# A state-space layer with a gated feed-forward: TensorE's column jobs in two halves, with one of a slot's two tiles of states transposed ahead of each

## The reference

```python
xn = _layernorm(x)
u, gate = split(xn @ W_in.T)                 # 1024 channels each
u = silu(causal_conv4(u) + conv_b)
dt, B, C = split(u @ Wx.T)                   # 32, 16, 16; each normalised (rms)
delta = softplus(dt @ Wdt.T + dt_bias)
state = exp(delta * A) * state + (delta * u) * B     # 1024 x 16 states, step by step
y = (sum over n of state * C + u * D_param) * silu(gate)
g = silu(ffn(xn))                            # gated feed-forward, 512 -> 1376 -> 512
out = x + (y @ W_out.T) * g
```

## Time and profile before

| what | value |
|---|---|
| median of three runs | 1201.54 us |
| the profiled execution | 1197.73 us, of which span 1195.9 us |
| PE busy | 1068.4 us (89%) |
| DVE busy | 1049.6 us (88%) |
| POOL busy | 1008.5 us (84%) |
| ACT busy | 710.2 us (59%) |
| granted TensorE clock, mean | 0.96 of full |

### The profile page before, as it was taken

One profiled execution on the slowest core, in us unless ns is written; L12 is line 12 of the kernel. 1 busy time (PEld: TensorE's weight loads), 2 busy tenths in 40 slices (PEclk: granted clock), 3 DMA queues, 4 the chain that ended last, 5 costly groups with the idle time before them and its releaser, 6 DMA issues.

```text
span 1195.9 us, 16709 instructions
## 1 busy us (share of the span) xinstructions
PE 1068.4 (89%) x5072; PEld 764.7 (64%) x5072; DVE 1049.6 (88%) x1248; ACT 710.2 (59%) x1155; POOL 1008.5 (84%) x542
## 2 busy tenths in 40 slices
PE   5979886888999979998997997998998999999767
PEld 4757665566657767675756786576756787555444
DVE  4478789899989999899987999899998999888985
ACT  4667646776574846577583665576576575464440
POOL 3589997999978898889977897879988889878961
PEclk9979998799999999999999998999999999999978
DMA  4537553443224443343322463424323443334410
GB/s 133 206 128 239 187 185 129 139 155 132 90 87 152 170 175 118 121 155 129 107 81 100 166 203 117 152 103 160 107 96 107 161 160 124 119 101 150 141 61 36
DMA packets 46566, 160.82 MB, mean 134 GB/s; under 512 B 5355, under 2 KB 5611, under 8 KB 37004
## 3 DMA queue, kind: packets, MB, share of 16 engines
q1 hardware_dynamic: 45424, 159.14, 38.9%
q10 hardware_dynamic: 1052, 0.59, 0.2%
HBM read 135.33 MB, written 24.38 MB: 134 GB/s over the span
## 4 chain that ended last, share of the span: by engine, by line
PE 47%; DVE 18%; POOL 16%; issue 14%; ACT 3%; DMA 1%; DVEq 1%; SPq 0%; POOLq 0%; ACTq 0%
PE pj L1068 15%; PE hT L1353 10%; DVE sb_h L1007 9%; POOL sb_dBu L770 8%; PE pj L1266 7%; DVE sb_yT L934 4%; PE pj L1300 4%; PE pj L1331 3%; POOL sb_yT L740 3%; PE pj L1086 2%; PE pj L1371 2%; DVE sb_un L855 2%; POOL sb_un L714 1%; POOL sb_w_sp L709 1%; PE pj L1073 1%
## 5 line engine op out<-in xcount | busy, mean ns | idle before, releaser
L770 POOL TENSOR_TENSOR sb_dBu<-sb_v,sb_bb 128x1024 f32<-128x1024 f32 x256 | 606.8, 2382 | 34.1 <-DVE sb_h L1007 26.6
L1007 DVE TENSOR_TENSOR_SCAN sb_h<-dA,sb_dBu 128x512 f32<-128x512 f32 x512 | 596.2, 1205 | 42.1 <-POOL sb_dBu L770 29.2
L581 ACT ACTIVATE dA<-sb_delta,sb_apar 128x512 f32<-128x512 f32 x512 | 345.0, 688 | 252.8 <-DVE sb_h L1007 248.6
L1068 PE MATMUL pj<-sb_x_hi,sb_w_sp 128*128 128x512 f32 x1208 | 347.6, 411 | 22.8 <-DVE sb_un L855 12.0
L1353 PE MATMUL hT<-sb_ident,sb_h 128*128 128x128 f32 x2048 | 290.0, 284 | 83.2 <-DVE sb_yT L934 68.1
L1353 PEld LDWEIGHTS hT<-sb_ident,sb_h 128*128 128x128 f32 x2048 | 244.4, 145 | 167.6 <-DVE sb_yT L934 52.9
L1068 PEld LDWEIGHTS pj<-sb_x_hi,sb_w_sp 128*128 128x128 f32 x1208 | 222.2, 194 | 85.4 <-issue 23.4
L934 DVE SCALAR_TENSOR_TENSOR sb_yT<-hT,sb_cs,sb_yT 128x512 f32<-128x512 f32 x321 | 228.4, 732 | 46.1 <-PE hT L1353 45.5
L740 POOL TENSOR_TENSOR sb_yT<-sb_yT,sb_part 128x512 f32<-128x512 f32 x155 | 198.8, 1283 | 68.0 <-ACT sb_part L674 67.8
L674 ACT ACTIVATE sb_part<-hT,sb_cs_act 128x512 f32<-128x512 f32 x155 | 106.0, 684 | 160.2 <-PE hT L1353 151.9
L1068 PE MATMUL pj<-sb_x_lo,sb_w_sp 128*128 128x512 f32 x604 | 167.6, 400 | 0.0
(11 more groups left out here) (119 smaller groups left out, 816.4 us busy)
## 6 DMA issues: line engine op xcount, KB each, us to landing
sb_w_sp<-w_cache SPq DMA_DIRECT2D x55, 1024.0 KB, 4.8
sb_ring<-w_ring SPq DMA_DIRECT2D x67, 512.0 KB, 3.4
sb_bb<-b_rows SPq DMA_DIRECT2D x128, 256.0 KB, 3.7
w_cache<-sb_w_sp SPq DMA_DIRECT2D x19, 1024.0 KB, 4.8
sb_xio<-x SPq DMA_DIRECT2D x7, 1024.0 KB, 7.2
out<-sb_xio SPq DMA_DIRECT2D x3, 1024.0 KB, 5.7
sb_xio<-x SPq DMA_DIRECT2D x4, 256.0 KB, 3.7
out<-sb_xio SPq DMA_DIRECT2D x4, 256.0 KB, 2.0
```

Source lines behind the costliest of these rows:

```text
L581: nc.scalar.activation(dA[g % 2][:, :], delta[:, j, :], ACT.Exp, scale=apar[:, j, n:n + 1]).then_inc(dA_done, 1)
L770: nc.gpsimd.tensor_tensor(dBu[:, dbu_buffer(s), :, :], v[:, j:j + 2, :], bb[:, i % B_RING, :].unsqueeze(1).to_broadcast([P, 2, T]), ALU.mu ...
L1007: nc.vector.tensor_tensor_scan(h[:, i % 2, 2 * part + e, :], dA[g % 2][:, :], dBu[:, dbu_buffer(s), e, :], 0.0, ALU.mult, ALU.add).then_in ...
L1068: done = nc.tensor.matmul(bank[:, :], w[:, kk * P:(kk + 1) * P], xs[:, kk, :], start=(p == 0), stop=(p == len(products) - 1))
```

## The change

`column(s)` gets a second argument `half` and is called twice. The slot is now: first tile, `misc(s)`, half 0 of the column; second tile, half 1. `misc` is not divided. Of a column from `x` a half is six of the twelve products, of the out-projection two of four, of the down-projection the first two and what is left. All waits of a column stand in half 0, all signals at the last product. The u column at slot 31 gets one wait more at its head, for the new `x` (`xT_done`). `tail(s)` is called whole in half 1.

```diff
-            def from_x(bank, buf, part, ready, new_x=None):
+            def from_x(bank, buf, part, ready, new_x=None, halves=(0, 1)):
                 hi, lo = w_hi[:, buf, part], w_lo[:, buf, part]
                 products = [(w, xs, kk) for w, xs in ((lo, x_hi), (hi, x_lo), (hi, x_hi)) for kk in range(KH)]
                 for p, (w, xs, kk) in enumerate(products):
+                    if p // 6 not in halves:
+                        continue
...
-                done.then_inc(ready, 1)
+                if 1 in halves:
+                    done.then_inc(ready, 1)
...
-                        for m in range(JH):
+                        for m in (2 * half, 2 * half + 1):
...
-                        if part == 1:
+                        if part == 1 and half == 1:
                             done.then_inc(op_ps, 1)
                     if last:
-                        tail(s)
+                        if half == 1:
+                            tail(s)
                         return
                     if s in U_AT:
                         j = U_AT.index(s)
...
+                        elif j == 0:
+
+                            pe.wait_ge(xT_done, (b + 1) * KH + 3)
...
                     if s in DOWN_AT:
                         e, ts = DOWN_AT[s]
+                        ts = ts[:2] if half == 0 else ts[2:]
...
                         done.then_inc(hT_ps, 1)
-                    misc(s)
-                    column(s)
+                        if c % 2 == 0:
+                            misc(s)
+                        column(s, c % 2)
```

More of the change, by code:

```diff
@@ L1216, in misc, with ffn @@
                         to_delta(b + 1, j, pj[3])
-                def ffn(c, q):
+                def ffn(c, q, half):
                     t, part = q // 2, q % 2
-                    if part == 0:
+                    if half == 0 and part == 0:
                         weights(c, FFN0 + t)
-                    if q < 3 and isinstance(c, int) and c == 0:
+                    if half == 1:
+                        pass
+                    elif q < 3 and isinstance(c, int) and c == 0:
                         pe.wait_ge(*[(sg_done, 3), (sg_done, 4), (del_done, 2)][q])
@@ L1232, in ffn, with column @@
                         pe.wait_ge(fs_done, c * KI + t)
-                    from_x(pj[q % 3], t % HI_RING, part, fu_ps if part else fg_ps)
-                def column(s):
+                    from_x(pj[q % 3], t % HI_RING, part, fu_ps if part else fg_ps, halves=(half,))
+                def column(s, half):
                     if s - q_ffn < 2 * KI:
-                        ffn(b, s - q_ffn)
+                        ffn(b, s - q_ffn, half)
                     if s >= SLOTS - LEAD and not last:
-                        ffn(b + 1, s - SLOTS + LEAD)
+                        ffn(b + 1, s - SLOTS + LEAD, half)
                     j = s - q_gate1 + JH
                     if JH <= j < KD:
-                        if j % 2 == 0:
+                        if half == 0 and j % 2 == 0:
                             weights(b, GATE1 + (j - JH) // 2)
-                        if j == JH:
+                        if half == 1:
+                            pass
+                        elif j == JH:
                             pe.wait_ge(f_done, (b + 1) * KI - 1)
@@ L1252, in column @@
                             pe.wait_ge(sg_done, b * KD + JH + 1)
-                        from_x(pj[(Q_GATE1 + j - JH) % 3], (GATE1 + (j - JH) // 2) % HI_RING, j % 2, gt_ps)
+                        from_x(pj[(Q_GATE1 + j - JH) % 3], (GATE1 + (j - JH) // 2) % HI_RING, j % 2, gt_ps, halves=(half,))
                     e, part = (s - S_OUT) // 2, (s - S_OUT) % 2
                     if 0 <= e < KH and not first:
-                        if part == 0:
+                        if part == 0 and half == 0:
                             weights(b, OUT0 + e)
@@ L1274, in column @@
                         j = U_AT.index(s)
-                        if j % 2 == 0:
+                        if half == 0 and j % 2 == 0:
                             weights(b, U0 + j // 2)
-                        if j == 1 and first:
+                        if half == 1:
+                            pass
+                        elif j == 0:
+                            pe.wait_ge(xT_done, (b + 1) * KH + 3)
+                        elif j == 1 and first:
                             pe.wait_ge(sg_done, 7)
@@ L1282, in column @@
                             pe.wait_ge(tap_done, ((b + 1) * KD + j - 1) * (KC - 1))
-                        from_x(pj[U_BANK[j % 2]], (GATE1 + 2 + j // 2) % HI_RING, j % 2, u_ps, (b + 1) * KH if j == 0 else None)
+                        from_x(pj[U_BANK[j % 2]], (GATE1 + 2 + j // 2) % HI_RING, j % 2, u_ps, (b + 1) * KH if j == 0 else None, (half,))
                     if s in DOWN_AT:
                         e, ts = DOWN_AT[s]
-                        if e == 0 and ts[0] == 0:
+                        ts = ts[:2] if half == 0 else ts[2:]
+                        if 0 not in ts:
+                            pass
+                        elif e == 0:
                             pe.wait_ge(f_done, (b + 1) * KI)
@@ L1291, in column @@
                                 pe.wait_ge(og_done, b * KH)
-                        elif e == 1 and ts[0] == 0:
+                        elif e == 1:
                             pe.wait_ge(g_done, b * KH + 1)
-                        elif ts[0] == 0:
+                        else:
                             pe.wait_ge(sg_done, (b + 1) * KD + e)
@@ L1306, in column @@
                         j = GATE0_AT.index(s)
-                        if j % 2 == 0:
+                        if half == 0 and j % 2 == 0:
                             weights(b, GATE0 + j // 2)
-                        if j < 2:
+                        if half == 1:
+                            pass
+                        elif j < 2:
                             pe.wait_ge(tap_done, ((b + 1) * KD + 7 + j) * (KC - 1))
@@ L1314, in column @@
                             pe.wait_ge(sg_done, (b + 1) * KD + 1)
-                        from_x(pj[GATE0_BANK[j]], (GATE1 + 6 + j // 2) % HI_RING, j % 2, gt_ps)
+                        from_x(pj[GATE0_BANK[j]], (GATE1 + 6 + j // 2) % HI_RING, j % 2, gt_ps, halves=(half,))
                 def tail(s):
```

## The result

The changed kernel took 1249.44 us (median of four runs, 1242.74 to 1251.28), against 1201.55 us for the kernel before: ratio 1.0394, interval 1.0355 to 1.0432, 48 us slower. Forecast were 1225 us and a range of 1203 to 1242. The direction and the place (VectorE standing behind late tiles) were right, the size (23 us) was half of what it is, and 1249 lies above the range.

A forecast was written before the change was run, and what follows sets the result against it. Three nearly full engines (TensorE 89%, VectorE 88%, GpSimd 84%), none bounding the whole alone. Terms of 7.05, twice 7.55 and 1.0 us summed to 23.2, giving 1224.7 beside the median; predicted 1225 us, range 1203 to 1242.

The forecast's parts named there:

- (a): Delta jobs of the first slots: VectorE waits for a later tile, 0.5 us a middle batch (bounds 0 and 1.6).
- (b): Start of the out-projection: second tile no longer done during a wait, 0.5 us a batch, none in the first.
- (c): From out-projection to taps, slot 33: tile 2.16 us later, VectorE full after it; 2.1 us a middle batch.
- (d): Inside the taps stretch, slots 35, 36 and 39: late second tiles, 1.8 us halved to 0.9 a middle batch.
- (e): Slots 47 and 48: 16 `to_ssm` products each ahead of the second tile, 2.9 us a middle batch (bounds 0 and 3.9).
- (f): Slots 55 to 57: delta job and two down products ahead of the tile, 1.3 us halved to 0.65 a middle batch.
- More alternations: Every slot: one more switch between transposes and products on TensorE, costed at zero, at most 28 us.
- The wait that goes: TensorE's 20 waits ahead of four transposes, 18.6 us together, could go; net effect taken as about zero.
- would show it: Expected signs: VectorE's wait for transposes from 45.5 to 80 us or more, about 2.5 us of wait in slot 33.
- more than the sum: Rival: unhalved terms plus 1.2 GHz stretches after TensorE's waits, signed by four transposes taking 0.66 us; 1239 us, chance 0.13.
- the ScalarE reserve: Delta jobs of the first slots: VectorE's 1.03 us wait for ScalarE at 695.52 was counted as covering delay, leaving 0.5 us.

The follow-up runs named there:

- experiment 7: New order only in slots 45 and 63, old order elsewhere, against the kernel before: 1204.81 us, ratio 1.0040.
- experiment 5: Changed kernel plus six unused products on TensorE ahead of the wait for GpSimd's last block of `u` in slot 47: 1234.05 us, ratio 1.0287 to the kernel before.
- experiment 4: Changed kernel with slots 47 and 48 put back in the old order (both tiles ahead): 1240.05 us, ratio 1.0349 to the kernel before.
- experiment 6: New order only in slots 32 to 46, old order elsewhere, against the kernel before: 1219.85 us, ratio 1.0180.
- experiment 8: Changed kernel with VectorE's side work moved ahead of the slot's second add, except in slots 0 and 1: 1231.11 us, ratio 1.0270 to the kernel before.
- experiment 11: Old order except new in slots 35 to 46, VectorE's side work ahead of its second add in slots 37 to 48, six unused products in slot 47: 1197.39 us.
- experiment 2: Changed kernel with only `misc` ahead of the second tile, the whole column behind it: 1210.51 us, ratio 1.0080 to the kernel before.
- experiment 9: Old order on TensorE throughout, VectorE's side work ahead of the second add from slot 2 on, against the kernel before: 1211.39 us, ratio 1.0111.

## Why the prediction was wrong

The terms of the sum beside the rows of the ledger, each added up over the four batches (us):

| term | in the sum | in the ledger |
|---|---|---|
| start and turns, to slot 5 | 0 | 5.6 |
| (a) | 2.0 | 7.6 |
| (b) | 1.5 | 8.2 |
| (c) | 6.3 | 5.8 |
| (d) | 2.7 | 12.7 |
| (e) | 8.7 | 9.8 |
| (f) | 2.0 | 4.3 |
| together | 23.2 | 54.0 |

So the mechanism was right, and these steps of the sum failed: (d), which was halved and had no term for slot 40 (10 us short); slot 18 beside (b), put at nothing (5.4 us); the wait for ScalarE that (a) counted as a reserve ((a) is 5.6 us short); the start, put at nothing; and (f), halved (2.3 us short). (e) comes within 1.1 us, and that is luck, as told below.

*More alternations, zero.* Right. Slot 33 takes 4.74 us in both kernels, an out-projection slot 4.31 us in both.

*The wait that goes, zero.* Right: experiment 7 picks it out and wins nothing. (One of the 20 waits, 0.81 us at 642.84, stands ahead of a first tile.)

*(b) and (c), 0.5 and 2.1 us.* The mechanisms were right in size. The first out-projection slot's successor starts 0.44 us later relative to the job before it (slot 23 to 24: TensorE's difference grows from 35.55, the delay of the gate silu that releases the job, to 35.99 us), and the add of slot 34 is 2.3 us further behind than TensorE. What "would show it" was partly wrong: I expected one wait of 2.5 us in slot 33, and the lateness came in earlier and in parts: +0.5 us in slot 24, +1.2 in slot 25 (VectorE's wait of 1.32 us at 795.77), +0.4 in each of slots 32 and 33. The measured 2.5 us of stretch (b) are another thing: slot 18, which I left out. After the layernorm statistics TensorE has waited 4.65 us and runs at 1.2 GHz in both kernels (before, too: its tiles of slot 18 took 1.97 us for eight at 728.18), but now half a column at that clock, 2.7 us, stands ahead of the second tile. That is +1.8 us. The first batch has it too, four slots later, as its layernorm statistics stand four slots later: +1.8 us in slot 22, where the granted clock was 0.50 in both kernels.

*(d), 1.8 halved to 0.9.* In the third batch each of the two slots costs +0.93 us, as worked out; the halving was wrong, since GpSimd took nothing up. Not foreseen: slot 40, +1.7 us, whose column waited 2.46 us for taps and then ran at 1.2 GHz ahead of the second tile (granted clock 0.65 over the slot); and small steps, mostly of 0.1 to 0.2 us a slot, +1.1 together. It is the clock that costs in slot 40, not the wait. In the third batch of experiment 5's kernel the same wait was followed by a clock of 1.0, and the slot cost 0.1 us. TensorE's timeline there:

```profile
857.00 1.20 PE L1075 MATMUL pj<-sb_x_hi,sb_w_sp 128*128 128x512 f32 x4 [2.46 <-DVE sb_un L859]
858.04 0.62 PE L1075 MATMUL pj<-sb_x_lo,sb_w_sp 128*128 128x512 f32 x2
```

The changed kernel and those of experiments 4, 5 and 6 have this wait (2.45 or 2.46 us) in all of their twelve slots 40: seven cost 1.4 to 1.7 us, five 0.1 to 0.2.

In slots 35 to 42 the second tile now lands just when VectorE wants it (0.13 us before the add, where the kernel before had 1.7 to 3.9 us). This closes a ring: taps, half column, tile, add, next taps. Experiments 8 and 11 cut it, by doing the taps ahead of the add, and the whole loss of (d) goes.

*(a), 0.5 (bounds 0 and 1.6).* It measured 1.6 to 3.2 in the last three batches and 0.0 in the first. The step that failed is "at 695.52 VectorE waits 1.03 us for ScalarE anyway". That wait is not a reserve, for ScalarE's decay waits for VectorE's scans. ScalarE's timeline, the kernel before and then the changed one:

```profile
687.57 1.31 ACT L581 ACTIVATE dA<-sb_delta,sb_apar 128x512 f32<-128x512 f32 x2
...
720.56 0.69 ACT L581 ACTIVATE dA<-sb_delta,sb_apar 128x512 f32<-128x512 f32 x1 [1.42 <-DVE sb_h L1007]
721.67 0.69 ACT L581 ACTIVATE dA<-sb_delta,sb_apar 128x512 f32<-128x512 f32 x1 [0.42 <-DVE sb_h L1007]
```

ScalarE ran these two decays without a wait and now waits 1.42 and 0.42 us for scans. So it is late as well, and VectorE's wait for it grew from 1.03 to 1.79 us, in the row that answers to the earlier trace rows:

```profile
718.04 0.75 DVE L934 SCALAR_TENSOR_TENSOR sb_yT<-hT,sb_cs,sb_yT 128x512 f32<-128x512 f32 x1 [1.30 <-PE hT L1372]
...
729.00 2.34 DVE L1007 TENSOR_TENSOR_SCAN sb_h<-dA,sb_dBu 128x512 f32<-128x512 f32 x2 [1.79 <-ACT dA L581]
```

*(e), 2.9 us.* The late tile is as said: at full clock VectorE waits 2.96 us (experiment 5). Its price was wrong twice over, in opposite directions, and that the total of 9.8 us is near the 8.7 charged is luck. I took 1.0 us of it as covered, and 3.4 us are (experiment 5), so at 2.4 GHz the term is zero. And I took for granted that the ssm slots run at 2.4 GHz; in both middle batches slot 48 ran at 1.2 GHz and took 8.4 us instead of 4.4, all of it ahead of a tile. So 10.8 us were measured in two batches where the mechanism alone gives none, and experiment 5 takes them away. The rival "more than the sum" had the clock, but for four transposes after a wait, not for 32 records with a tile behind them; and its sign for it was misread, since 0.66 us is the busy time of four transposes, which at 2.4 GHz is 0.60 us without a wait, and 0.44 us is their pace. The Trainium skill bears on it ("TensorE: Matmul & The Clock Gate", section "HAM oscillation — how this bites in real kernels": waits inside a loop can throw the array back to half clock, time and again); the case that the Trainium skill tells there has longer waits, for transfers. The trace agrees in kind, with waits of 1.19 us ahead of both falls, but experiment 2 has like waits with a fall (0.93 us) and without one (0.94). What decides in a given batch stays open.

*(f), 1.3 halved to 0.65.* It measured 1.3 to 1.6. Here the unhalved term was right.

*Start and end.* The first batch opens 4.1 us later, a term that I had not priced (3.5 of it in slot 0). The five kernels with the changed order in slot 0 stand there between +2.4 and +3.7 us, those with the old order between -0.8 and +2.2, so some 2.5 us are the order and the rest is scatter. Its slots to 23 cost 2.6 us, though it has no out-projection: 1.8 of them are slot 22 (above), and I have no experiment on the rest. The last batch cost 4.1 us instead of 1.0, of which 3.2 are (a).

The sum for the third batch with the rows unhalved and without the ScalarE reserve is 1.6 + 0.5 + 2.1 + 1.8 + 1.3 = 7.3 us, plus (e) at 1.2 GHz 5.6, slot 18 1.8 and slot 40 1.7: 16.4. The last three (9.1 us) are taken from the trace after and were not foreseen. Measured between slot 5 of the third batch and slot 5 of the last were 18.5.

## What to carry to other kernels

A wait of the engine behind (VectorE for ScalarE, 1.03 us) covers a delay only if what it waits for is not itself released by the delayed work; follow the releaser one step further back before it is counted as slack, and where a row gives a number, don't halve it out of caution (in (d) and (f) the unhalved number is what came). A result that another engine's in-order list needs belongs ahead of the work that may run at the lower clock, for in such a stretch everything before it counts double. Where a late operand can't be avoided, put the consumer's independent work ahead of it: that took away all of (d). Only there, though: put in every slot of the old order, it cost 12 us (experiment 9).

## What the runs showed of the hardware

Products of 64 columns on a TensorE that had been at 2.4 GHz: 32 records in 3.68 us at a granted clock of 1.0 and 6.93 us at 0.50. Six products of 512 columns in place of the wait ahead of them kept 2.4 GHz in all twelve pairs of ssm slots of the four profiled runs that had them. In the ten profiled kernels without them the clock fell in ten of thirty pairs, behind waits of 0.75 to 2.13 us; it stayed up in the other twenty, behind waits of up to 1.86 us.

One of VectorE's smallest operations can be its most expensive. Timelines of the kernel before, third batch, VectorE and GpSimd:

```profile
869.16 2.48 DVE L870 TENSOR_SCALAR sb_ms<-sb_ms 128x4 f32<-128x4 f32 x1
...
870.32 1.29 POOL L740 TENSOR_TENSOR sb_yT<-sb_yT,sb_part 128x512 f32<-128x512 f32 x1
```

and of the changed kernel:

```profile
920.05 0.17 DVE L870 TENSOR_SCALAR sb_ms<-sb_ms 128x4 f32<-128x4 f32 x1
...
920.37 2.28 POOL L704 TENSOR_TENSOR sb_ms<-sb_ms,sb_half 128x12 f32<-128x12 f32 x1 [1.19 <-DVE sb_ms L871]
```

Four elements a partition take 2.48 us where GpSimd is at work without a gap (its instructions end at 871.61, VectorE's at 871.64), and 0.17 us where GpSimd stands idle. "SBUF — State Buffer" of the Trainium skill, section "SBUF: two separate sides", has it as a shared pair of ports that GpSimd and some forms of VectorE's instructions need, and whichever starts first holds for its whole instruction. The trace agrees: the two ends lie 0.03 us apart. It also shows that the end of one GpSimd instruction, at 870.32 with the next one right behind it, did not let VectorE in. It is what hid (e) at full clock: a VectorE that is late finds GpSimd idle, and gets 2.3 us back.
